# Three shared chunks ahead of the expert blocks and one beside the final sums, in place of two and two

## The chip, the cores and the metric

The kernel runs on one core of one Trainium2 chip. The metric is the device time of one execution in microseconds (us), lower being better. TensorE is called PE, VectorE DVE, ScalarE ACT, GpSimd POOL and SyncE SP below, as the profile calls them. Each engine works through its own list of instructions in the order written; between engines there are only semaphores.

## The reference, cut to what matters

A four-layer network on x of 2048 tokens by 256 features. Each layer adds an attention part and then a feed-forward part. The change lies in the last layer's feed-forward part, a mixture of 16 experts of which each token uses two, plus a shared network that every token goes through:

```python
shared = jnp.einsum('bls,ds->bld',
    jax.nn.silu(jnp.einsum('bld,sd->bls', x, sfc1)) * jnp.einsum('bld,sd->bls', x, sfc2), sfc3)
logits = jnp.einsum('bld,ed->ble', x, gate_w)
top_w, top_idx = jax.lax.top_k(logits, TOP_K)
top_w = jax.nn.softmax(top_w, axis=-1)
...
h = jax.nn.silu(jnp.einsum('td,ehd->teh', xf, w1))
moe = jnp.einsum('teh,te,edh->td', h, dispatch, w2)
return moe.reshape(B, L, D) + shared
...
x = x + jnp.tanh(g_ffn[3]) * _L3_ffn_ref(_layernorm(x, axis=-1), ...)
```

Here x is normalised, each sfc matrix has 512 hidden features, and each expert has 128.

## The kernel before, in words

The order of all work is written out by hand: for each stage there is one function for each engine. The last stage is `pe_ffn3`, `act_ffn3`, `dve_ffn3`, `pool_ffn3` and `sp_ffn3`, followed by `sp_end`. The 2048 tokens are 16 tiles of 128. All data are float32. The stage goes like this.

**Routing.** DVE picks two experts for each token and works out a slot for each of the 4096 (token, expert) pairs; the slots of one expert fill whole blocks of 128 rows, 47 blocks in all (NB3). POOL then writes the normalised tokens into a DRAM buffer xb3 by those slots: 32 indirect DMAs in `pool_scatter` (L718), one tile of one choice each.

**Shared chunks.** The shared network is made in four chunks of 512 tokens (`pe_shared`, `act_shared`, `dve_shared`, with c from 0 to 3). PE makes for each of four groups of 128 hidden features two 128x512 products (L149 is the helper `mm` that issues every matmul), ACT takes a sigmoid of the first (L2267), and DVE multiplies twice (L2274 and L2276) into HS. Then PE makes four 128x256 products, and DVE adds each, times the layer's gate, into x (L2279), which counts s_yd. Two pairs of PSUM banks alternate between the feature groups, so that PE can be two groups ahead of DVE and no more (the wait on s_hs, n - 1).

**Expert blocks.** For each of the 47 blocks SP loads 128 rows from xb3 (L2229; the first waits until all 32 scatters have landed; four buffers, so that load j waits for the transpose of block j - 4). PE transposes them (`turn`, L2296), ACT copies (`keep`, L2353), PE multiplies by the expert's first matrix, whose number it reads into a register (`up`), ACT takes the sigmoid (L2363), DVE multiplies (L2403), PE transposes again (`lift`, L2313), DVE copies (L2410), PE multiplies by the second matrix (`down`), ACT copies (L2371) and SP writes the 128 rows to a DRAM buffer yb3 (L2239). The blocks use all eight PSUM banks, so PE's shared chunks stand wholly before or behind them, and waits on s_hs and s_yd guard the change-over.

**Final sums.** When the last block has been written to yb3, POOL gathers for each tile its two expert rows: 32 indirect DMAs in `pool_gather` (L723). There are 8 buffers, so four tiles are in flight, and the gathers of tile t wait for the sum of tile t - 4 (s_fx). DVE adds each gathered tile into x with its weight (L2418), two instructions a tile, and SP then writes that tile out (L2448).

What sets the order around the change is DVE's and PE's written order. PE has chunks 0 and 1, then 47 blocks, then chunks 2 and 3. DVE has chunks 0 and 1, its share of the blocks, then chunk 2, sums of tiles 0 to 7, chunk 3, sums of tiles 8 to 15.

Of the kernel before, what the change touches and what calls it, by code (L numbers as in the profile page):

```python
# [6 lines left out]
ALU = mybir.AluOpType  # L7
# [9 lines left out]
NT = 16  # L17
# [35 lines left out]
def settle(e, own, ins):  # L53

    own.n += 1
    ins.then_inc(own.sem, 1)
    e.wait_ge(own.sem, own.n)
# [20 lines left out]
def build(nc, d, out):  # L78
    with ExitStack() as ctx:
# [12 lines left out]
        dve, act, pool = Own(sem("dve")), Own(sem("act")), Own(sem("pool"))  # L92
# [45 lines left out]
        xs = lambda t: X[:, t, :]  # L138

        s_w3, s_fx = sem("w3_in"), sem("x_out")  # L140
# [489 lines left out]
        s_gth = sems("gathered", 8)  # L630
# [112 lines left out]
        s_dn, s_yd = sem("down_prod"), sem("y_ready")  # L743
# [1470 lines left out]
        f3_Lg, f3_W12 = view(f3_w + 3200, NT, 16), view(f3_w + 3456, 2, NT)  # L2214
# [6 lines left out]
        f3_G = view(oW + 4096, 8, 256)  # L2221
# [40 lines left out]
        def act_shared(e, c):  # L2262
            for n in range(4 * c, 4 * c + 4):
                e.wait_ge(s_up, 64 + 2 * n + 1)
                if n >= 2:
                    e.wait_ge(s_hs, n - 1)
                e.activation(f3_S1[:, n % 2, :], psum[:, 2 * (n % 2) + 2, :], ACT.Sigmoid).then_inc(s_sg, 1)  # L2267
# [14 lines left out]
        def pe_ffn3(e):  # L2282
            pe_turn_logits(e, 7, lambda i: (s_xn, 113 + 2 * i + 2), xn, sml("wg3"), 16)
            pe_ranks(e, 3, 16, 32, f3_w)
            pe_totals(e, 16, 32, f3_w)
            e.wait_ge(s_w3, 32)
            e.wait_ge(s_er, 2)
            for c in range(2):
                pe_shared(e, c)

            def turn(j):
                e.wait_ge(s_rin[j % 4], RIN3[j % 4] + 16 * (j // 4 + 1))
                if j >= 2:
                    e.wait_ge(s_bx, 23 + j - 1)
                for k in range(2):
                    m = e.transpose(psum[:, j % 2, 128 * k:128 * k + 128], f3_XG[:, j % 4, 128 * k:128 * k + 128], ident)  # L2296
                m.then_inc(s_bt, 1)

            def up(j):
                e.wait_ge(s_bx, 23 + j + 1)  # L2300
                if j >= 2:
                    e.wait_ge(s_bh_, 23 + j - 1)
                regs[j] = e.value_load(ER[0:1, j:j + 1], min_val=0, max_val=15)
                for k in range(2):
                    m = mm(e, psum[:, 2 + j % 2, 0:128], f3_XGT[:, j % 3, k, :],
                           f3_W1[:, bass.ds(regs[j], 1), k, :].rearrange("p e n -> p (e n)"), k == 0, k == 1)
                m.then_inc(s_bu, 1)

            def lift(j):
                e.wait_ge(s_bh_, 23 + j + 1)  # L2310
                if j >= 2:
                    e.wait_ge(s_ba, 23 + j - 1)
                e.transpose(psum[:, 4 + j % 2, 0:128], f3_H[:, j % 2, :], ident).then_inc(s_bl, 1)  # L2313

            def down(j):
                e.wait_ge(s_ba, 23 + j + 1)
                e.wait_ge(s_bo, 23 + j - 1) if j >= 2 else e.wait_ge(s_yd, 48)
                mm(e, psum[:, 6 + j % 2, 0:256], f3_HTT[:, j % 2, :],
                   f3_W2[:, bass.ds(regs[j], 1), :].rearrange("p e n -> p (e n)"), True, True).then_inc(s_bd, 1)

            regs = {}
            e.wait_ge(s_hs, 8)
            turn(0)
            turn(1)
            e.wait_ge(s_wm, 192)
            for j in range(NB3 + 2):
                if j < NB3:
                    up(j)
                if j + 2 < NB3:
                    turn(j + 2)  # L2330
                if 1 <= j <= NB3:
                    lift(j - 1)
                if 2 <= j:
                    down(j - 2)
            e.wait_ge(s_bh_, 23 + NB3)
            e.wait_ge(s_ba, 23 + NB3)
            e.wait_ge(s_bo, 23 + NB3)
            for c in range(2, 4):
                pe_shared(e, c)

        def act_ffn3(e):
            for i in range(8):
                act_turn(e, 7, i)
            e.wait_ge(s_gx, 3)
            e.activation(f3_GW, f3_GW, ACT.Exp).then_inc(s_ge, 1)
            for c in range(2):
                act_shared(e, c)

            def keep(j):
                e.wait_ge(s_bt, 23 + j + 1)  # L2350
                if j >= 3:
                    e.wait_ge(s_bu, 46 + j - 2)
                e.activation(f3_XGT[:, j % 3, :, :].rearrange("p k n -> p (k n)"), psum[:, j % 2, 0:256],  # L2353
                             ACT.Copy).then_inc(s_bx, 1)

            keep(0)
            keep(1)
            for j in range(NB3 + 2):
                if j < NB3:
                    e.wait_ge(s_bu, 46 + j + 1)  # L2360
                    if j >= 2:
                        e.wait_ge(s_bh_, 23 + j - 1)
                    e.activation(f3_SGM[:, j % 2, :], psum[:, 2 + j % 2, 0:128], ACT.Sigmoid).then_inc(s_bg, 1)  # L2363
                if j + 2 < NB3:
                    keep(j + 2)
                if j >= 2:
                    y = j - 2
                    e.wait_ge(s_bd, 23 + y + 1)
                    if y >= 3:
                        e.wait_ge(s_rout[y % 3], ROUT3[y % 3] + 16 * (y // 3))  # L2370
                    e.activation(f3_Y[:, y % 3, :], psum[:, 6 + y % 2, 0:256], ACT.Copy).then_inc(s_bo, 1)  # L2371
            for c in range(2, 4):
                act_shared(e, c)

        def dve_ffn3(e):
            e.wait_ge(s_x, 112)
            for t in range(NT):
                dve_norm(e, 113 + t + 1, t)
            PL = psum[:, 0, 0:256].rearrange("p (t e) -> p t e", t=NT)
            e.wait_ge(s_lg, 3)  # L2380
            settle(e, dve, e.tensor_copy(f3_Lg, PL))
            OH, M_, MI = dve_top(e, f3_Lg, 16, 2, f3_w)
            e.tensor_tensor(f3_GW, M_[:, 1, :], M_[:, 0, :], ALU.subtract).then_inc(s_gx, 1)
            dve_scan(e, OH, 16, 32, f3_w)
            e.wait_ge(s_ge, 3)
            settle(e, dve, e.tensor_scalar(f3_W12[:, 0, :], f3_GW, 1.0, None, ALU.add))
            settle(e, dve, e.reciprocal(f3_W12[:, 0, :], f3_W12[:, 0, :]))
            settle(e, dve, e.tensor_scalar(f3_W12[:, 0, :], f3_W12[:, 0, :], TG[:, 7:8], None, ALU.mult))
            e.tensor_tensor(f3_W12[:, 1, :], f3_W12[:, 0, :], f3_GW, ALU.mult)
            V1 = dve_blocks(e, 2, 16, NB3, f3_w)  # L2390
            e.sem_inc(s_er, 1)
            e.wait_ge(s_rk, 3)
            dve_pick(e, OH, V1, 16, 32, f3_w, f3_SLOT)
            settle(e, dve, e.tensor_copy(f3_SLI, f3_SLOT))
            e.sem_inc(s_slot, 1)  # L2395
            for c in range(2):
                dve_shared(e, c)
            for j in range(NB3 + 1):
                if j < NB3:
                    e.wait_ge(s_bg, 23 + j + 1)  # L2400
                    if j >= 2:
                        e.wait_ge(s_bl, 23 + j - 1)
                    e.tensor_tensor(f3_H[:, j % 2, :], psum[:, 2 + j % 2, 0:128], f3_SGM[:, j % 2, :],  # L2403
                                    ALU.mult).then_inc(s_bh_, 1)
                if j >= 1:
                    y = j - 1
                    e.wait_ge(s_bl, 23 + y + 1)
                    if y >= 2:
                        e.wait_ge(s_bd, 23 + y - 1)
                    e.tensor_copy(f3_HTT[:, y % 2, :], psum[:, 4 + y % 2, 0:128]).then_inc(s_ba, 1)  # L2410
            for c in range(2):
                dve_shared(e, 2 + c)
                for t in range(8 * c, 8 * c + 8):
                    e.wait_ge(s_yd, 40 + t + 1)
                    for k in range(2):
                        s = (2 * t + k) % 8
                        e.wait_ge(s_gth[s], 96 + 16 * (t // 4 + 1))
                        m = e.scalar_tensor_tensor(out=xs(t), in0=f3_G[:, s, :], scalar=f3_W12[:, k, t:t + 1], in1=xs(t),  # L2418
                                                   op0=ALU.mult, op1=ALU.add)
                        if k == 0:  # L2420
                            settle(e, dve, m)
                    m.then_inc(s_fx, 1)

        def pool_ffn3(e):
            e.wait_ge(s_slot, 3)
# [228 lines left out]
```

## Time and profile before

| what | us |
|---|---|
| median of 3 runs | 2287.68 (2282.6 to 2291.75) |
| the profiled execution, its own time | 2269.89 |
| its span, first to last instruction | 2268.0 |
| PE busy in the span | 1811.4 (80%) |
| DVE busy | 1194.7 (53%) |
| ACT busy | 880.3 (39%) |
| POOL busy | 838.9 (37%) |
| mean granted clock of PE, share of full | 0.88 |

The rows of the profile give times from the start of the span. Busy shares are averages over stages of very different kinds; the stage in question is the last some 200 us of the span, from about 2067 us on. A timeline row gives the start, the length, the engine and line, the operation, how many instructions were merged, and in brackets how long the engine had been idle before, and what released it. PE's lengths in such a row overlap at their ends, since matmuls are pipelined. DMA_INDIRECT on POOL is the time that POOL takes to describe the transfer, which then takes its own time to land.

### The profile page before, as it was taken

What the parts mean: (1) busy time and instruction counts of PE and PEld (TensorE: products, weight loads), DVE (VectorE), ACT (ScalarE), POOL (GpSimd) and SP (SyncE); (2) the same over time, 40 slices, a digit from 0 to 9 for tenths busy, and PEclk for the clock granted to TensorE, in tenths of its full rate; (3) what the DMA queues carried; (4) which work ended last, traced back from release to release, by engine and by line L of the source; (5) the groups of instructions that cost most, each with busy time, mean ns of one, the idle gap of its engine ahead of it and who ended that gap; (6) DMA issues with size and microseconds to landing.
All of it is one profiled execution on the core that took longest, in us unless ns stands there. A gap on an engine that the chain in (4) does not pass through costs nothing.

```text
span 2268.0 us, 25730 instructions
## 1 busy us (share of the span) xinstructions
PE 1811.4 (80%) x9072; PEld 1125.0 (50%) x9072; DVE 1194.7 (53%) x2217; ACT 880.3 (39%) x1365; POOL 838.9 (37%) x805
## 2 busy tenths in 40 slices
PE   6643999908875688885899577799999899987895
PEld 3343998904653322245455345554445545555653
DVE  5942444453758466662111669656664566633334
ACT  3112433303325677741122155455453455421440
POOL 2133000071347444433000445355565456643114
PEclk9856999958977699996899899699999999987997
DMA  9112223030000000032111200000000000011443
GB/s 368 53 61 77 91 100 118 20 93 0 1 18 1 1 1 1 1 149 106 40 35 33 94 1 1 28 1 1 1 1 1 0 1 1 1 75 47 137 129 93
DMA packets 60076, 112.22 MB, mean 49 GB/s; under 512 B 7829, under 2 KB 51288, under 8 KB 57520
## 3 DMA queue, kind: packets, MB, share of 16 engines
q1 hardware_dynamic: 52272, 90.02, 11.3%
q0 software_dynamic: 7680, 20.57, 2.8%
q8 instruction: 76, 1.25, 0.2%
q14 instruction: 48, 0.39, 0.1%
HBM read 71.12 MB, written 39.80 MB: 49 GB/s over the span
## 4 chain that ended last, share of the span: by engine, by line
PE 61%; DVE 17%; POOL 9%; issue 5%; ACT 5%; DMA 3%; SPq 0%; POOLq 0%; DVEq 0%; ACTq 0%
PE psum L149 57%; POOL xb L718 3%; POOL arena L1519 2%; DVE arena L2027 2%; POOL arena L723 2%; ACT arena L1318 2%; PE psum L183 1%; DVE arena L460 1%; DVE arena L154 1%; DVE arena L164 1%; DMA arena<-yb,arena 1%; DMA arena<-xb 1%; POOL arena L620 1%; DVE arena L1400 1%; DVE rounded L759 1%
## 5 line engine op out<-in xcount | busy, mean ns | idle before, releaser
L149 PE MATMUL psum<-arena 128*128 128x512 f32 (+20 forms) x5127 | 1223.6, 468 | 178.1 <-DVE arena L1434 30.6
L149 PEld LDWEIGHTS psum<-arena 128*128 128x128 f32 (+6 forms) x5127 | 602.1, 172 | 689.1 <-issue 448.8
L149 PE MATMUL psum<-rounded 128*128 128x270 f32 (+6 forms) x2688 | 491.1, 336 | 34.6 <-DVE rounded L759 19.6
L149 PEld LDWEIGHTS psum<-rounded 128*128 128x128 f32 (+3 forms) x2688 | 382.3, 189 | 146.7 <-issue 48.0
L2100 POOL TENSOR_TENSOR arena<-arena 128x1024 f32<-128x1024 f32 (+1 forms) x112 | 270.6, 2416 | 152.7 <-ACT arena L2069 148.1
L723 POOL DMA_INDIRECT arena<-yb,arena x80 | 78.4, 980 | 390.1 <-DMA yb<-arena 343.8
L2069 ACT ACTIVATE arena<-psum 128x1024 f32<-128x1024 f32 x144 | 147.3, 1023 | 190.8 <-PE psum L149 190.1
L2027 DVE TENSOR_REDUCE arena<-psum 128x1 f32<-128x512 f32 x256 | 164.1, 684 | 86.8 <-PE psum L149 85.7
L1318 ACT ACTIVATE arena<-psum,arena 128x1024 f32<-128x1024 f32 (+1 forms) x192 | 156.3, 909 | 47.5 <-PE psum L149 47.4
L1535 POOL TENSOR_TENSOR arena<-arena 128x256 f32<-128x256 f32 x128 | 94.2, 757 | 131.5 <-ACT arena L1318 130.5
L718 POOL DMA_INDIRECT xb<-arena x80 | 80.3, 1004 | 114.9 <-DVEq L2395 37.8
L191 ACT ACTIVATE arena<-psum 128x512 f32<-128x512 f32 x56 | 32.2, 596 | 219.3 <-PE psum L183 219.3
L183 PE MATMUL psum<-arena 128*128 128x128 f32 x224 | 45.4, 355 | 81.5 <-DVE arena L964 53.7
L759 DVE SCALAR_TENSOR_TENSOR rounded<-arena,rounded 128x540 fp32r<-128x540 f32 (+1 forms) x96 | 82.0, 886 | 33.6 <-ACT rounded L889 32.1
L883 ACT ACTIVATE arena<-psum,arena 128x540 f32<-128x540 f32 x64 | 45.4, 710 | 129.9 <-PE psum L149 127.1
L159 POOL TENSOR_SCALAR arena<-arena 128x1 f32<-128x1 f32 x113 | 24.3, 215 | 177.8 <-DVE arena L155 171.9
L183 PEld LDWEIGHTS psum<-arena 128*128 128x128 f32 x224 | 36.8, 196 | 91.4 <-DVE arena L964 54.2
L1965 DVE SCALAR_TENSOR_TENSOR rounded<-psum,rounded 64x512 fp32r<-64x512 f32 (+1 forms) x80 | 47.2, 590 | 63.2 <-ACT rounded L1943 51.0
L164 DVE TENSOR_SCALAR arena<-arena 128x256 f32<-128x256 f32 x128 | 61.3, 494 | 24.7 <-POOL arena L160 23.8
L2097 POOL TENSOR_TENSOR arena<-arena 128x1024 f32<-128x1024 f32 x16 | 38.0, 2375 | 83.2 <-ACT arena L2069 83.2
L957 DVE TENSOR_TENSOR arena<-psum,arena 128x256 f32<-128x256 f32 (+1 forms) x40 | 16.9, 422 | 94.7 <-PE psum L149 94.7
L1674 POOL MEMSET arena<- 128x1 f32 x1 | 0.1, 98 | 179.8 <-DMA yb<-arena 179.8
(245 smaller groups left out, 1918.8 us busy)
## 6 DMA issues: line engine op xcount, KB each, us to landing
arena<-in_w SPq DMA_DIRECT2D x8, 2048.0 KB, 8.0
yb<-arena SPq DMA_DIRECT2D x102, 128.0 KB
xb<-arena SPq DMA_DIRECT2D x5, 2048.0 KB, 17.6
arena<-xb SPq DMA_DIRECT2D x70, 128.0 KB, 2.2
arena<-in_w1u SPq DMA_DIRECT2D x4, 2048.0 KB, 14.0
arena<-xb SPq DMA_DIRECT2D x8, 512.0 KB
arena<-in_w1d SPq DMA_DIRECT2D x1, 4096.0 KB, 13.5
arena<-in_w3b SPq DMA_DIRECT2D x1, 4096.0 KB, 12.5
```

Of the source, the lines that this page charges most:

```text
L149: return e.matmul(o, l, r, start=start, stop=stop, skip_group_check=True)
L164: e.tensor_scalar(xn(t), src(t), MV[:, t, 0:1], RS[:, t:t + 1], ALU.subtract, ALU.mult).then_inc(s_xn, 1)
L183: m = e.transpose(pt[:, t, k, :], src(2 * i + t)[:, 128 * k:128 * k + 128], ident)
L718: e.indirect_dma_start(buf, bass.IndirectOffsetOnAxis(idx[:, c:c + 1], 0), src(c % NT), None, bounds_check=bound, oob_is_err=False).then_i ...
L723: e.indirect_dma_start(dst, None, buf, bass.IndirectOffsetOnAxis(idx[:, col:col + 1], 0)).then_inc(s_gth[s], 16)
L759: e.scalar_tensor_tensor(out=dst, in0=src, scalar=1.0, in1=hi, op0=ALU.mult, op1=ALU.subtract).then_inc(sig, 1)
L1318: e.activation(PT[:, u % 3, 2 * h:2 * h + 2, 0:n], psum[:, bk:bk + 2, 0:n], ACT.Exp, bias=NBD[:, 0:1]).then_inc(s_ae, 1)
L1535: e.tensor_tensor(PT[:, u % 3, 2 * h:2 * h + 2, 0:128], PT[:, u % 3, 2 * h:2 * h + 2, 0:128], bc(cst("caus"), 1, 2), ALU.mult).then_inc(s_ ...
L1965: e.scalar_tensor_tensor(out=lo, in0=psum[r, bk, 0:64 if (kind, c) == ("k", 2) else 512], scalar=1.0, in1=hi, op0=ALU.mult, op1=ALU.subtra ...
L2027: m = e.tensor_reduce(x3_MX[:, t, a, c:c + 1], psum[:, bk, :], AX.X, ALU.max)
L2069: e.activation(x3_P[0:rows, g % 4].rearrange("p a n -> p (a n)"), psum[0:rows, bk:bk + 2, :].rearrange("p a n -> p (a n)"), ACT.Exp, scale ...
L2100: m = e.tensor_tensor(ac, ac, x3_P[0:rows, g % 4], ALU.add)
```

## The change

One more shared chunk (c = 2) is made ahead of the expert blocks, on all three engines, and only chunk 3 stays behind them. The counts that the change-over waits for rise with it (s_hs from 8 to 12, s_yd from 48 to 52). DVE's final sums, which were split in two halves with chunk 3 between them, become one run of 16 tiles behind chunk 3. Nothing is computed more or less often, and POOL's and SP's lists stay the same.

```diff
@@ pe_ffn3
-            for c in range(2):
+            for c in range(3):
                 pe_shared(e, c)
...
-                e.wait_ge(s_bo, 23 + j - 1) if j >= 2 else e.wait_ge(s_yd, 48)
+                e.wait_ge(s_bo, 23 + j - 1) if j >= 2 else e.wait_ge(s_yd, 52)
...
-            e.wait_ge(s_hs, 8)
+            e.wait_ge(s_hs, 12)
...
-            for c in range(2, 4):
-                pe_shared(e, c)
+            pe_shared(e, 3)
@@ act_ffn3
-            for c in range(2):
+            for c in range(3):
                 act_shared(e, c)
...
-            for c in range(2, 4):
-                act_shared(e, c)
+            act_shared(e, 3)
@@ dve_ffn3
-            for c in range(2):
+            for c in range(3):
                 dve_shared(e, c)
...
-            for c in range(2):
-                dve_shared(e, 2 + c)
-                for t in range(8 * c, 8 * c + 8):
-                    e.wait_ge(s_yd, 40 + t + 1)
-                    for k in range(2):
-                        s = (2 * t + k) % 8
-                        e.wait_ge(s_gth[s], 96 + 16 * (t // 4 + 1))
-                        m = e.scalar_tensor_tensor(out=xs(t), in0=f3_G[:, s, :], scalar=f3_W12[:, k, t:t + 1], in1=xs(t),
-                                                   op0=ALU.mult, op1=ALU.add)
-                        if k == 0:
-                            settle(e, dve, m)
-                    m.then_inc(s_fx, 1)
+            dve_shared(e, 3)
+            for t in range(NT):
+                e.wait_ge(s_yd, 40 + t + 1)
+                for k in range(2):
+                    s = (2 * t + k) % 8
+                    e.wait_ge(s_gth[s], 96 + 16 * (t // 4 + 1))
+                    m = e.scalar_tensor_tensor(out=xs(t), in0=f3_G[:, s, :], scalar=f3_W12[:, k, t:t + 1], in1=xs(t),
+                                               op0=ALU.mult, op1=ALU.add)
+                    if k == 0:
+                        settle(e, dve, m)
+                m.then_inc(s_fx, 1)
```

## Rows read from the trace of the kernel before

**Rows 1.** The profile's page: the span and the engines' busy time.
```profile
...
span 2268.0 us, 25730 instructions
...
PE 1811.4 (80%) x9072; PEld 1125.0 (50%) x9072; DVE 1194.7 (53%) x2217; ACT 880.3 (39%) x1365; POOL 838.9 (37%) x805
...
```

**Rows 2.** Timeline of PE, last layer: start, length, line, operation, count [idle before, releaser].
```profile
...
2106.84 7.17 PE L149 MATMUL psum<-arena 128*128 128x256 f32 x32 [0.85 <-DVE arena L2276]
2115.09 0.41 PE L2296 MATMUL psum<-arena 128*128 128x128 f32 x2 [1.08 <-DMA arena<-xb]
2115.94 0.44 PE L2296 MATMUL psum<-arena 128*128 128x128 f32 x2 [0.43 <-DMA arena<-xb]
2116.83 0.71 PE L149 MATMUL psum<-arena 128*128 x4 [0.45 <-issue]
...
2192.46 1.21 PE L149 MATMUL psum<-arena 128*128 x4
2194.30 13.97 PE L149 MATMUL psum<-arena 128*128 128x512 f32 x32 [0.63 <-issue]
...
2231.76 9.79 PE L149 MATMUL psum<-arena 128*128 128x512 f32 x16 [8.59 <-DVE arena L2276]
...
```

**Rows 3.** Chain of waits, 2110 to 2122 us: start, us, what.
```profile
...
2110.58 2.43 DMA xb<-arena
...
2113.40 2.50 DMA arena<-xb
...
```

**Rows 4.** Timeline of POOL, last layer: scatters (L718) and gathers (L723).
```profile
...
2070.81 1.11 POOL L718 DMA_INDIRECT xb<-arena  x1 [37.76 <-DVEq L2395]
...
2110.58 0.97 POOL L718 DMA_INDIRECT xb<-arena  x1 [0.30 <-issue]
2196.70 0.99 POOL L723 DMA_INDIRECT arena<-yb,arena  x1 [85.14 <-DMA yb<-arena]
...
2218.00 0.95 POOL L723 DMA_INDIRECT arena<-yb,arena  x1 [11.54 <-DVE arena L2418]
2219.25 1.13 POOL L723 DMA_INDIRECT arena<-yb,arena  x1 [0.30 <-issue]
...
2228.19 0.95 POOL L723 DMA_INDIRECT arena<-yb,arena  x1 [0.30 <-DVE arena L2418]
...
2233.19 0.95 POOL L723 DMA_INDIRECT arena<-yb,arena  x1 [0.30 <-issue]
...
2251.27 0.95 POOL L723 DMA_INDIRECT arena<-yb,arena  x1 [13.39 <-DVE arena L2418]
...
2260.20 0.95 POOL L723 DMA_INDIRECT arena<-yb,arena  x1 [0.30 <-issue]
```

**Rows 5.** Timeline of ACT, last layer: first sigmoid of chunks 2 and 3.
```profile
...
2196.29 0.60 ACT L2267 ACTIVATE arena<-psum 128x512 f32<-128x512 f32 x1 [2.20 <-PE psum L149]
...
2218.05 0.60 ACT L2267 ACTIVATE arena<-psum 128x512 f32<-128x512 f32 x1 [10.87 <-PE psum L149]
...
```

**Rows 6.** Groups of instructions, 2115 to 2194 us: PE's transposes of the expert blocks.
```profile
...
L2296 PE MATMUL psum<-arena 128*128 128x128 f32 x94 | 18.8, 283 | 2.2 <-DMA arena<-xb 2.1
...
```

**Rows 7.** By stretch: length, PE, PEld, DVE, ACT, POOL busy, clock, DMA share, GB/s.
```profile
...
2114.00:2116.00 2.00, 0.49 (x4) 0.27 (x4) 0.48 (x1) 0.38 (x1) 0.00 (x0) 1.00 0.78 240
...
2118.00:2120.00 2.00, 2.00 (x9) 2.00 (x10) 0.60 (x3) 0.80 (x3) 0.00 (x0) 0.50 0.29 67
...
2122.00:2124.00 2.00, 2.00 (x16) 1.59 (x14) 0.73 (x4) 1.66 (x6) 0.00 (x0) 1.00 0.35 97
...
```

**Rows 8.** Timeline of DVE, last layer: final sums (L2418) and chunk 3's first product (L2274).
```profile
...
2216.74 3.75 DVE L2418 SCALAR_TENSOR_TENSOR arena<-arena 128x256 f32<-128x256 f32 x8
...
2222.57 0.48 DVE L2418 SCALAR_TENSOR_TENSOR arena<-arena 128x256 f32<-128x256 f32 x1 [0.87 <-DMA arena<-yb,arena]
...
2230.20 0.68 DVE L2274 TENSOR_TENSOR arena<-psum,arena 128x512 f32<-128x512 f32 x1
...
```

**Rows 9.** Busy time and granted clock behind PE's long wait (columns as in rows 7).
```profile
...
2232.00:2235.00 3.00, 3.00 (x4) 1.23 (x5) 0.90 (x2) 0.00 (x0) 2.39 (x3) 0.50 0.47 134
...
```

## The prediction, made before the changed kernel ran

> **What bounds the kernel now.** I read the page first. The span is 2268.0 us, and PE is busy for 80% of it [rows 1]. That is an average over all layers; the change touches only the last stage, so I went to the timelines of the four engines there and asked, at each place where work leaves or arrives, who is waiting for whom.
>
> The head of the stage, PE's timeline: chunk 1's last matmuls start at 2106.84 and end 7.17 us later, at 2114.01. PE then waits 1.08 us for a DMA, transposes, waits 0.43 us for the next DMA, transposes, and starts the first expert product at 2116.83 [rows 2]. The DMAs waited for are the first loads from xb3. The chain shows why they come then: the last scatter lands 2.43 us after 2110.58, and the load takes 2.50 us from 2113.40 [rows 3]. So two shared chunks fill PE's time under the 32 scatters almost exactly. PE finishes 1.1 us before the blocks' data are there. A third chunk finds no gap to fill.
>
> The middle: PE has the expert blocks until 2193.67 (2192.46 + 1.21) [rows 2]; their timing depends on their start only.
>
> The tail: POOL's gathers start at 2196.70, 3.0 us behind PE's last block; POOL issues eight and then waits 11.54 us, until 2218.00, for the first sum, which on DVE stands behind chunk 2. From 2218.00 it issues at an even pace, and before 2251.27 it waits once more, 13.39 us, for sums that stand behind chunk 3 [rows 4]. PE, meanwhile, can run only two feature groups of chunk 3 ahead of DVE and then waits 8.59 us, until 2231.76, for it [rows 2]. So in the tail DVE's written order makes POOL and PE wait in turn. The tail is 2268.0 - 2193.67 = 74.33 us long.
>
> **The change part by part.**
>
> The price of one chunk: from chunk 2's first sigmoid to chunk 3's is 2218.05 - 2196.29 = 21.76 us, with PE the engine that sets it [rows 5].
>
> Head: chunk 2 is added between 2114.01 and the blocks, +21.76. The loads have then long landed (SP issues four without asking PE), so PE's DMA waits of 1.08 and 0.43 us go, -1.51 [rows 2]. What is late next is nothing: the second transpose, ACT's copy, the register read and the first product follow as before. Head: +20.25 us. Nothing covers it, since no other engine has work that the blocks wait for. POOL's scatters are finished, and DVE and ACT run beside PE in the chunk. SP's list is unchanged. Its four first loads are issued under the chunk, and the fifth waits for PE's first transpose as before.
>
> Within the blocks the trace could give something back. All four stalls of PE on a load come to 2.1 us, the first two (1.51) among them [rows 6]; the other 0.6 us I leave in. And PE's granted clock, at 1.00 until 2116, is at 0.50 from 2118 to 2120 (1.2 of 2.4 GHz), just behind the short waits of the change-over, and back at 1.00 by 2122 [rows 7]. With PE busy until the first transpose this dip may be gone. At most 4 us ran at half clock, so 2 us is the most that it can give back, and it is less if part of a block's time is hand-overs between engines. The new change-over still has the same small gaps between transposes and products, so I take 0 and keep 2 us for the low end.
>
> Tail, rebuilt from rows. From PE's last block to the first sum is one chunk, as now with chunk 2: 2216.74 - 2193.67 = 23.07 us [rows 2, 8]. Eight gathers have landed under it, as now. From the first sum to the ninth gather is 2218.00 - 2216.74 = 1.26 us. Then, in place of eight gathers, chunk 3 and eight more with their waits, 24 gathers run through. Twelve took 2233.19 - 2218.00 = 15.19 us beginning with the stretch in which DVE had only sums, up to 2230.20 [rows 4, 8]. That is 11 steps of 1.25 and one of 1.43. Twenty-three steps at 1.25, with 0.18 for that one, are 28.93 us. From the last gather's issue to the end is 2268.0 - 2260.20 = 7.80 us [rows 1, 4]. The sum is 23.07 + 1.26 + 28.93 + 7.80 = 61.06 us against 74.33, so -13.27 us. That contains the end of PE's wait of 8.59 us and of the half clock behind it: from 2232 to 2235, as the products of chunk 3 resume, the clock is 0.50 [rows 9].
>
> Could the sums set the pace, not POOL? Two buffers of each tile come free with its sum; tile 4's second sum ends at 2222.57 + 0.48 = 2223.05 [rows 8], and the gather that needs it is issued at 2228.19 [rows 4]. There are 5 us of slack, and it does not shrink, since eight sums cost DVE 3.75 us, 0.94 a tile [rows 8], and POOL's two gathers 2.5. PE, ACT and the yb3 writes have nothing left in that stretch. The writes of the finished tiles run beside the gathers, but they do so in the twelve-gather stretch already.
>
> **Sum:** +20.25 - 13.27 = +6.98 us. Against the profiled execution that is a span of 2268.0 + 7.0 = 2275.0, and 2269.89 + 7.0 = 2276.9 us for its own time. The median of the runs, 2287.68, lies 17.8 us above that execution, and nothing in one trace says where; I add the difference to the median: 2294.7 us, or 0.31% more. The sign comes from lost overlap: taking a chunk out of the tail gives back only 13.3 of its 21.8 us, since the rest lay beside gathers, and in front it lies beside nothing.
>
> **The rivals.**
>
> Rival 1, sums get in the way of gathers (slower still). The gather at 2219.25 took 1.13 us, not 0.95, while eight sums ran back to back on DVE [rows 4, 8]. If sums beside POOL's work cost every one of the 24 gathers that 0.18 us, not one of them, the tail is 23 x 0.18 = 4.1 us longer and the change costs +11.1 us, 2298.8 us. Against it: in the stretch after 2220 sums and gathers alternate at 1.25 us a gather. A harder form holds each of 23 gathers for a whole sum, 0.48 us [rows 8]: 7.0 + 11.0 = +18.0 us, 2305.7 us. The trace speaks for it in at most one gather of twelve. The Trainium skill ("SBUF — State Buffer", section "SBUF: two separate sides") states the harder form as a rule: while DVE runs an operation that takes both of its SBUF port pairs, GpSimd is locked out and cannot write the descriptors of its DMAs. By it the 1.13 us would be the normal case, and the twelve-gather stretch disagrees.
>
> Rival 2, the added chunk is hidden (faster). If the scatters' landing, and not PE, set the start of the blocks, chunk 2 would fill waiting time and the tail's 13.3 us would be a gain. Break-even is where the first load lands 7 us later against PE than in this trace, that is 8 us after chunk 1's end; fully hidden, at 20 us later, it would give 2287.7 - 13.3 = 2274.4 us. The 32 scatters are issued 1.28 us apart, from 2070.81 to 2110.58 [rows 4]. The unprofiled runs are 17.8 us longer than the profiled one; if 8.0 of these sat in the scatters (0.25 us in each), the change would be worth 7.0 - 8.0 = -1.0 us, 2286.7. Nothing in the trace shows such a delay: the last scatter, too, follows the one before it after 0.30 us.
>
> Rival 3, the blocks run better with their loads in hand. If the other 0.6 us of load stalls went and the clock dip's 2 us too, the change would cost 7.0 - 2.6 = +4.4 us, 2292.1. For it: four loads are ready at the start, and PE comes to the change-over without a wait. Against: from the fifth on each load still waits for a transpose, as now.
>
> **How the numbers follow.** Chances: the forecast's sum, +6 to +8 us, 0.68; rival 1 at +11 us 0.09 and at +18 us 0.03; rival 3, 0.13; rival 2, 0.07. About 0.5% (11.4 us) is what a measurement of this kernel can tell from no change, and three runs of one program spread over 9 us. The forecast lies 4.4 us inside that bound, so of its 0.68 a good 0.1 may be measured beyond it; of rival 1's 0.12 some 0.07. That gives slower by over 0.5% 0.18, faster by over 0.5% 0.04 (part of rival 2), within 0.5% 0.78. The range reaches from rival 2's break-even side, 2286, to rival 1 with the spread of the runs, 2302.
>
> **What would show it right or wrong.** In the trace of the changed kernel: PE starts the first transpose without a DMA wait some 21.8 us behind chunk 1's end; first expert product near 2137.1; PE's last block ends near 2213.9; POOL's gathers start 3 us behind it, wait once, 11.5 us, and then 24 run in 29 us; no second wait of POOL, no 8.6 us wait of PE; the clock stays at 1.00 through the last chunk. The forecast is wrong if the first transpose still waits for a load (rival 2), if many gathers take 1.1 us or are more than 1.3 us apart (rival 1), or if the 47 blocks take 2 us less than the 76.8 us from the first product to the last block's end (rival 3).

## The result and the profile after

| | us |
|---|---|
| before, median of 12 runs | 2287.87 (2282.6 to 2294.37) |
| changed, median of 12 runs | 2297.27 (2291.18 to 2303.59) |
| ratio | 1.004, 95% interval 1.0025 to 1.0055 |
| changed, profiled execution | 2295.21, span 2293.3 |

The changed kernel is slower by 0.4%, 5.7 to 12.6 us by the interval. The forecast was 2294.7 us and +7.0 us, with "within 0.5%" as the likeliest outcome. A second comparison on another chip (below) gave 1.003, 1.0009 to 1.0051.

The profile's page of the changed kernel, span and busy time, against [rows 1]: all engines have the same work to within 5 us, so the difference is waiting.

```profile
...
span 2293.3 us, 25730 instructions
...
PE 1815.7 (79%) x9072; PEld 1125.6 (49%) x9072; DVE 1196.0 (52%) x2217; ACT 879.9 (38%) x1365; POOL 840.2 (37%) x805
...
```

PE's timeline of the last stage, to be held against [rows 2]. The row with 32 products of 128x512 is where chunk 0 starts (at 2067.24 us in the first profile of before).

```profile
...
2064.88 16.99 PE L149 MATMUL psum<-arena 128*128 128x512 f32 x32 [3.69 <-issue]
2082.72 5.45 PE L149 MATMUL psum<-arena 128*128 128x256 f32 x24 [0.85 <-DVE arena L2276]
2095.34 10.27 PE L149 MATMUL psum<-arena 128*128 128x256 f32 x24 [7.17 <-issue]
2116.00 10.16 PE L149 MATMUL psum<-arena 128*128 128x512 f32 x16 [10.39 <-DVE arena L2276]
2127.01 20.91 PE L149 MATMUL psum<-arena 128*128 128x256 f32 x64 [0.85 <-DVE arena L2276]
2148.77 7.17 PE L149 MATMUL psum<-arena 128*128 128x256 f32 x32 [0.85 <-DVE arena L2276]
2155.78 0.60 PE L2296 MATMUL psum<-arena 128*128 128x128 f32 x4
2157.49 0.71 PE L149 MATMUL psum<-arena 128*128 x4 [1.11 <-ACT arena L2352]
...
2230.97 1.21 PE L149 MATMUL psum<-arena 128*128 x4
2232.81 13.97 PE L149 MATMUL psum<-arena 128*128 128x512 f32 x32 [0.63 <-issue]
2247.63 7.17 PE L149 MATMUL psum<-arena 128*128 128x256 f32 x32 [0.85 <-DVE arena L2276]
```

Three things can be read here. First, the third chunk stands ahead: the first transpose (2155.78) follows chunk 2's last product at once, with no wait for a load. Second, the tail is short: from the last block's end, 2230.97 + 1.21 = 2232.18, to the span's end are 61.1 us. Third, there is something that nobody forecast: PE waits 7.17 and 10.39 us in the middle of the chunks. POOL's gathers answer to [rows 4]: one wait of 11.52 us, and then 24 gathers in one run.

```profile
...
2235.21 0.99 POOL L723 DMA_INDIRECT arena<-yb,arena  x1 [125.96 <-DMA yb<-arena]
...
2256.51 0.94 POOL L723 DMA_INDIRECT arena<-yb,arena  x1 [11.52 <-DVE arena L2415]
...
2285.51 0.95 POOL L723 DMA_INDIRECT arena<-yb,arena  x1 [0.30 <-issue]
```

The third thing again, on the engines that PE waited for. First the waits of 2080 to 2160 us (engine, line, releaser: us in total, times, longest), where "remote" is what the profile writes when no engine or queue that it sees released the instruction; then DVE's timeline.

```profile
...
ACT arena L2267 <- remote: 33.0, 1, 33.0
...
DVE arena L2279 <- remote: 26.8, 3, 17.1
...
```

```profile
...
2085.52 0.48 DVE L2279 SCALAR_TENSOR_TENSOR arena<-psum,arena 128x256 f32<-128x256 f32 x1 [2.86 <-PE psum L149]
2094.70 0.48 DVE L2279 SCALAR_TENSOR_TENSOR arena<-psum,arena 128x256 f32<-128x256 f32 x1 [8.70 <-remote]
2112.26 0.49 DVE L2279 SCALAR_TENSOR_TENSOR arena<-psum,arena 128x256 f32<-128x256 f32 x1 [17.07 <-remote]
2113.75 0.48 DVE L2279 SCALAR_TENSOR_TENSOR arena<-psum,arena 128x256 f32<-128x256 f32 x1 [1.00 <-remote]
...
```

PE had made the products of chunk 0's first three tiles by 2088.17 (2082.72 + 5.45), about 1.7 us apart, but DVE added them at 2085, 2094 and 2112. PE needs those adds for its next tile, so its wait of 7.17 us ends with DVE's late add of the second tile. The sigmoid at 2113.80 and the one behind it had both their products by 2105.61 (2095.34 + 10.27). All this ends soon after the scatters do: POOL's last scatter is issued at 2108.27. This costs 22.5 us: from the start of chunk 0 to the end of the last chunk ahead are 91.06 us here and 68.53 us in the second profile of the same kernel. PE's two waits are 17.6 us of that; the other 5 go with the granted clock, which is at 0.50 behind both of them (2092 to 2098 and 2110 to 2122 us). So this one profile (+25.3 us on the span) is no measure of the change.

What DVE and ACT waited for can be read from the trace's record of semaphore updates. Each last matmul of an add's product raises a count (s_dn) that DVE waits for:

```text
                         matmul ends                          count raised
changed, second          2082.04 2083.77 2085.50 2087.22      2082.06 2083.78 2085.51 2087.24
changed, first           2084.71 2086.44 2088.16 2098.74      2085.50 2094.68 2112.24 2113.72
```

In the second profile the count comes 0.01 to 0.02 us behind the matmul, and so it does in the other eleven. Here it comes 0.8, 8.2, 24.1 and 15.0 us behind it, and each add starts 0.02 to 0.03 us after its count. The count that ACT waits for behaves alike: the products of chunk 1's first two feature groups end from 2100.46 to 2105.61, and all four are counted between 2113.78 and 2113.96. So DVE and ACT did not stop by themselves: PE's counts reached them late. Why they were late this does not show.

To set executions side by side, I took every profile apart at the same four marks. The start of the stage itself moves from 2062 to 2075 us between executions, whatever the kernel, since the layers ahead of it take more or less time. A comparison within the stage is free of that. "Head" is from chunk 0's first product to the first expert product, "blocks" from there to the last block's end, "tail" from there to the span's end.

```text
profile                        head   blocks   tail   stage
before, first                 49.59   76.84   74.33   200.76
before, second                49.74   76.22   74.58   200.54
before, third                 49.85   77.11   74.04   201.00
before, fourth                49.61   76.07   74.70   200.38
changed, first                92.61   74.69   61.12   228.42   (the nameless wait)
changed, second               70.08   76.66   61.15   207.89
changed, third                70.09   76.20   61.11   207.40
changed, fourth               68.57   75.05   61.11   204.73
tail alone                    49.74   76.93   61.05   187.72
woven, two and two            49.80   75.73   51.11   176.64
woven, three and one          70.09   76.71   50.96   197.76
woven, one and three          49.90   77.32   69.84   197.06
woven, one sum earlier        49.72   76.31   50.41   176.44
```

The mean stage of before is 200.67 us, and that of the changed kernel's three undisturbed profiles 206.67: +6.0 us, by head +19.9, blocks -0.6, tail -13.3.

### The profile page after: what moved, and what is told of

It is laid out like the page before. It is cut to its first block, busy times and chain, and to the rows that moved or that the text cites. A ratio compares the mean times of both kernels' runs of the same rounds, so it can differ in the third digit from the quotient of the medians.

```text
span 2293.3 us, 25730 instructions
## 1 busy us (share of the span) xinstructions
PE 1815.7 (79%) x9072; PEld 1125.6 (49%) x9072; DVE 1196.0 (52%) x2217; ACT 879.9 (38%) x1365; POOL 840.2 (37%) x805
## 4 chain that ended last, share of the span: by engine, by line
PE 63%; DVE 15%; POOL 7%; ACT 5%; issue 5%; DMA 2%; another core or an unknown queue 1%; SPq 0%; POOLq 0%; DVEq 0%; ACTq 0%
PE psum L149 59%; POOL arena L1519 2%; POOL arena L723 2%; ACT arena L1318 2%; DVE arena L2027 2%; POOL xb L718 1%; DVE arena L460 1%; PE psum L183 1%; DVE arena L154 1%; DVE arena L164 1%; DVE arena L1400 1%; POOL arena L620 1%; PE psum L530 1%; DVE rounded L759 1%
## 5 line engine op out<-in xcount | busy, mean ns | idle before, releaser
L149 PE MATMUL psum<-arena 128*128 128x256 f32 (+20 forms) x5127 | 1228.6, 469 | 185.0 <-DVE arena L1434 29.7
L149 PEld LDWEIGHTS psum<-rounded 128*128 128x128 f32 (+3 forms) x2688 | 381.8, 189 | 147.0 <-issue 48.1
L723 POOL DMA_INDIRECT arena<-yb,arena x80 | 78.5, 981 | 417.7 <-DMA yb<-arena 384.4
L718 POOL DMA_INDIRECT xb<-arena x80 | 80.5, 1007 | 115.7 <-DVEq L2393 37.8
L183 PE MATMUL psum<-arena 128*128 128x128 f32 x224 | 43.8, 346 | 80.8 <-DVE arena L964 54.0
L160 POOL TENSOR_TENSOR arena<-arena 128x1 f32<-128x1 f32 x113 | 63.2, 559 | 9.4
## 6 DMA issues: line engine op xcount, KB each, us to landing
xb<-arena SPq DMA_DIRECT2D x5, 2048.0 KB, 17.6
```

The source lines that it names most:

```text
L149: return e.matmul(o, l, r, start=start, stop=stop, skip_group_check=True)
L160: e.tensor_tensor(RS[:, t:t + 1], VE[:, t:t + 1], cst("nhalf")[:, 0:1], ALU.pow).then_inc(s_rs, 1)
L183: m = e.transpose(pt[:, t, k, :], src(2 * i + t)[:, 128 * k:128 * k + 128], ident)
L718: e.indirect_dma_start(buf, bass.IndirectOffsetOnAxis(idx[:, c:c + 1], 0), src(c % NT), None, bounds_check=bound, oob_is_err=False).then_i ...
L723: e.indirect_dma_start(dst, None, buf, bass.IndirectOffsetOnAxis(idx[:, col:col + 1], 0)).then_inc(s_gth[s], 16)
```

## The experiments

**The two kernels once more.** Both unchanged, each profiled again three times; no edit. The question was the nameless wait: does it come with the change?

Expected of the second profile of before:

> The kernel before, unchanged, profiled once more. The changed kernel's profiled execution (2293.3 us span) holds a wait that the first profile of before does not: beside the 32 scatters, from 2082 to 2113 us, DVE's adds (L2279) and ACT's sigmoid (L2267) wait 26.8 and 33.0 us for something that the profile cannot name. Theory A (the wait belongs to the stage and not to the change; the one profile of before was a lucky execution, 18 us under its own median): this execution shows the same wait in the same place, chunk 1 ends about 20 us later than in the first profile, and the span is about 2283 to 2292 us. Rival B (the third chunk brings the wait with it): this execution again has no such wait, a span near 2268 us, and chunk 1 ends 47 us after chunk 0's first product.

Measured: 2273.21 us, span 2271.4, and no such wait. PE's timeline has the stage as in [rows 2], with the wait for the first load:

```profile
...
2070.86 16.98 PE L149 MATMUL psum<-arena 128*128 128x512 f32 x32 [3.69 <-issue]
...
2118.87 0.77 PE L2296 MATMUL psum<-arena 128*128 128x128 f32 x4 [1.24 <-DMA arena<-xb]
...
2197.45 13.97 PE L149 MATMUL psum<-arena 128*128 128x512 f32 x32 [0.63 <-issue]
...
```

Expected of the second profile of the changed kernel:

> The changed kernel once more. Theory A: the wait beside the scatters is there again, or, if it comes only in some executions, its absence gives a span of about 2275 us (2268.0 + 7.0). Rival B: always there, span 2290 to 2300 us. Both: the stretch from PE's last expert block to the end is 61.1 us, as forecast.

Measured: 2271.9 us, span 2270.1, and no such wait either. PE's timeline is the one that the forecast drew; the three chunks run without a gap, the first expert product stands 70.08 us behind chunk 0's start, and the last block ends at 2208.95:

```profile
...
2062.21 16.98 PE L149 MATMUL psum<-arena 128*128 128x512 f32 x32 [3.69 <-issue]
...
2123.57 7.17 PE L149 MATMUL psum<-arena 128*128 128x256 f32 x32 [0.85 <-DVE arena L2276]
2130.58 0.60 PE L2296 MATMUL psum<-arena 128*128 128x128 f32 x4
2132.29 0.71 PE L149 MATMUL psum<-arena 128*128 x4 [1.10 <-ACT arena L2352]
...
2207.74 1.21 PE L149 MATMUL psum<-arena 128*128 x4
2209.60 13.97 PE L149 MATMUL psum<-arena 128*128 128x512 f32 x32 [0.66 <-issue]
2224.43 7.17 PE L149 MATMUL psum<-arena 128*128 128x256 f32 x32 [0.85 <-DVE arena L2276]
```

POOL's timeline of the same execution, from the ninth gather to the last: 24 gathers whose starts span 28.99 us, with one of 1.13 us and all others near 0.95.

```profile
...
2233.30 0.95 POOL L723 DMA_INDIRECT arena<-yb,arena  x1 [11.53 <-DVE arena L2415]
2234.56 1.13 POOL L723 DMA_INDIRECT arena<-yb,arena  x1 [0.30 <-issue]
2235.99 0.95 POOL L723 DMA_INDIRECT arena<-yb,arena  x1 [0.30 <-DVE arena L2415]
...
2262.29 0.95 POOL L723 DMA_INDIRECT arena<-yb,arena  x1 [0.30 <-issue]
```

The stretches around the first blocks (length; PE, PEld, DVE, ACT, POOL busy with counts; granted clock; DMA share; GB/s) answer to [rows 7]. There the clock fell to 0.50 behind the change-over, and so it did in all four profiles of before. Here it stays at 1.00, as in all four of the changed kernel:

```profile
...
2130.00:2132.00 2.00, 1.18 (x8) 0.82 (x6) 0.48 (x1) 0.66 (x2) 0.00 (x0) 1.00 0.01 4
2132.00:2134.00 2.00, 1.55 (x11) 1.33 (x12) 0.29 (x1) 0.60 (x2) 0.00 (x0) 1.00 0.42 127
2134.00:2136.00 2.00, 1.70 (x13) 1.24 (x11) 0.72 (x4) 1.15 (x4) 0.00 (x0) 1.00 0.26 74
...
```

The third and fourth profiles:

> The kernel before, a third profile, to see whether the nameless wait beside the scatters ever comes without the third chunk. Theory A: it comes or not as it did for the changed kernel (one profile of two had it); if it comes, chunk 1 ends about 20 us late. Rival B: never here. Without it the stage from chunk 0's first product to the end takes 200.5 to 200.8 us, as in the two profiles so far.

Measured: 2268.13 us, stage 201.00, no such wait.

> The kernel before, once more, for the nameless wait that one profile of three of the changed kernel had and none of three of before. Theory A (it comes rarely and with either kernel): here or not; if not, the stage takes 200.5 to 201.0 us. Rival B (it needs the third chunk): not here.

Measured: 2276.09 us, stage 200.38, no such wait.

> The changed kernel once more, for the same wait. Theory A: as rare here as with before; without it the stage takes 207.4 to 207.9 us. Rival B: it comes again in a good part of the executions, with a stage of about 228 us.

Measured: 2274.68 us, stage 204.73, no such wait. The stage is 2.7 us shorter than the expected span of values; 1.5 us of it lie in the three chunks ahead (67.03 us, against 68.53), and 1.2 in the blocks. The clock goes with the first: it is back at 1.00 some 3 us into chunk 0, against 6 us in the second profile, and 3 us more at half clock are worth 1.5.

So rival B falls as a rule: three of four profiles of the changed kernel lack the wait. Theory A is not shown either, since none of four profiles of before has it, and no execution of any other kernel here. One in four against none in four tells nothing apart. Why PE's counts came late in that execution stays open.

**Timed again.** The changed kernel, run in turn with before on another chip.

> The changed kernel again, timed in turn with the kernel before, because the first comparison (+9.4 us, interval 0.25% to 0.55%) and the forecast's +7.0 us differ by less than the spread of the runs. Theory A (the nameless wait beside the scatters comes in some executions of either kernel): a median difference of 6 to 9 us; the stage from the first product of chunk 0 to the end takes 207.8 us in an execution without that wait. Rival B (the wait comes with the third chunk): the wait is there again in this profile, and the difference is 10 us or more.

Measured: 2279.96 us against 2270.32, ratio 1.003, interval 1.0009 to 1.0051 (+2.0 to +11.6 us); stage 207.40 us in its profile. The runs of both kernels spread over 15 us or more (before 2261.6 to 2276.57, changed 2266.86 to 2284.26), so the medians' difference of 9.6 us, just above the 6 to 9 expected, is a rough figure. The ratio of 1.003 is +6.8 us, and it agrees with the stage's +6.0. The wait is absent here.

**The tail alone.** Two chunks ahead as before, chunk 2 and the 16 sums behind the blocks as in the changed kernel, and chunk 3 left out:

```diff
-            for c in range(2, 4):
-                pe_shared(e, c)
+            pe_shared(e, 2)
...
-            for c in range(2):
-                dve_shared(e, 2 + c)
-                for t in range(8 * c, 8 * c + 8):
-                    e.wait_ge(s_yd, 40 + t + 1)
+            dve_shared(e, 2)
+            for t in range(NT):
+                e.wait_ge(s_yd, min(40 + t + 1, 52))
```

> Chunk 3 is left out, so that its 512 tokens lack the shared part; two chunks stand ahead as before, chunk 2 stands behind the blocks and the 16 sums run in one piece behind it. This is the change's tail with before's head. Forecast's sum: 13.3 us faster than before (2274.5), tail 61.1 us; and since the changed kernel adds only a chunk in front, it must be slower than this by the price of a chunk in front: 20.3 us if the chunk is paid in full. Rival (the chunk in front is partly hidden by the scatters): the gap to the changed kernel is well under 20 us.

Measured: 2261.19 us against 2273.87, ratio 0.9946 (0.9924 to 0.9968), so -12.3 us by the ratio, where -13.3 was forecast; stage 187.72 against 200.67, -13.0. (The times expected of this run and the next were reckoned from the first comparison's 2287.87 us. Before ran 14 us lower here, so the differences are what can be compared.) POOL's timeline has the one wait and the run behind it:

```profile
...
2204.78 0.99 POOL L723 DMA_INDIRECT arena<-yb,arena  x1 [85.40 <-DMA yb<-arena]
...
2226.08 0.95 POOL L723 DMA_INDIRECT arena<-yb,arena  x1 [11.54 <-DVE arena L2415]
...
```

The tail is 61.05 us, the changed kernel's. The stage of the changed kernel is 19.0 us longer than this on the mean (20.2, 19.7 and 17.0 in the three undisturbed profiles, the last with the shorter head): a chunk in front is paid nearly in full. The rival of a hidden chunk falls.

**Sums woven into the chunks.** If DVE's written order is what makes POOL and PE wait, another order should take the waits away with nothing moved ahead. The two chunks behind the blocks stay there. On DVE, p is a feature group's two products, a is the add of a tile's shared part, and t is a tile's final sum:

```diff
-            for c in range(2):
-                dve_shared(e, 2 + c)
-                for t in range(8 * c, 8 * c + 8):
...
+ORDER3 = ("p8 p9 p10 t0 p11 t1 t2 a8 t3 a9 t4 a10 t5 a11 t6 p12 t7 p13 t8 p14 t9 t10 p15 t11 a12 t12 a13 t13 a14 a15 t14 t15")
...
+            for what in ORDER3.split():
+                {"p": part, "a": add, "t": total}[what[0]](int(what[1:]))
```

> Two chunks ahead and two behind as before, but DVE's 16 sums are woven between the steps of chunks 2 and 3, each near the time at which its gathers land, so that POOL never waits long for a sum and PE never long for DVE. Theory (the tail is long because DVE's written order makes POOL and PE wait in turn): the tail falls from 74.3 us to 3.0 + 31 x 1.25 + 7.8 = 49.6 us, to 53 with small slips, so 21 to 25 us faster than before, 2263 to 2267 us. Rival (gathers, sums and chunk steps get in each other's way on DVE and on SBUF when they truly run together): gathers over 1.25 us apart, tail over 60 us, gain under 14 us.

Measured: 2251.23 us against 2273.87, ratio 0.9907 (0.9882 to 0.9931), -21.1 us by the ratio; stage 176.64, -24.0. PE's timeline of the tail, and POOL's:

```profile
...
2196.18 1.21 PE L150 MATMUL psum<-arena 128*128 x4
2198.06 13.97 PE L150 MATMUL psum<-arena 128*128 128x512 f32 x32 [0.67 <-issue]
2212.88 20.91 PE L150 MATMUL psum<-arena 128*128 128x256 f32 x64 [0.85 <-DVE arena L2418]
2234.64 7.17 PE L150 MATMUL psum<-arena 128*128 128x256 f32 x32 [0.85 <-DVE arena L2418]
```

```profile
...
2200.42 0.99 POOL L724 DMA_INDIRECT arena<-yb,arena  x1 [84.25 <-DMA yb<-arena]
...
2210.58 0.94 POOL L724 DMA_INDIRECT arena<-yb,arena  x1 [0.40 <-DVE arena L2430]
...
2214.01 0.94 POOL L724 DMA_INDIRECT arena<-yb,arena  x1 [1.24 <-DVE arena L2430]
...
2240.70 0.95 POOL L724 DMA_INDIRECT arena<-yb,arena  x1 [0.30 <-issue]
```

PE makes both chunks in 43.8 us (2198.06 to 2234.64 + 7.17) without the wait of 8.59 us of [rows 2]. POOL's waits of 11.54 and 13.39 us [rows 4] have shrunk to one of 1.24 us, and the last gather is issued 43.3 us behind the last block, where it was 66.5. The tail is 51.1 us. The theory stands: before, it was the order on DVE, not an engine, that made the tail long.

**Woven, three and one; woven, one and three.** With the tail near its floor of 49.6 us, the place of the chunks can be asked anew. The edits are the change's counts (s_hs 12, s_yd 52) on the woven kernel, and the opposite (one chunk ahead, s_hs 4, s_yd 44), each with its own order of sums.

> Three chunks ahead and one behind, as in the changed kernel, with the 16 sums woven between the steps of chunk 3. Theory (with woven sums the tail is set by 32 gathers, 31 x 1.25 us and what lies around them, so a chunk behind the blocks is free and a chunk ahead costs its full 20.3 us): tail 50 to 51.5 us, as with two chunks behind (51.1), and the whole 19 to 20.5 us slower than woven two and two, so 2 to 4 us faster than before. Rival (two chunks behind still cost something beside the gathers, or a third chunk ahead is partly hidden by the scatters): the gap to woven two and two is under 17 us.

Measured: 2264.11 us against 2270.32, ratio 0.9971 (0.9951 to 0.999), -6.6 us by the ratio. That is more than the 2 to 4 us expected, but the interval (2.3 to 11.1 us) holds most of them. The stage is 197.76, -2.9 us against before. Against woven two and two it is 21.1 us longer, 0.6 more than the most expected, of which the head is 20.3 and the blocks 1.0; the tail is the same (50.96 and 51.11). PE's tail now has a single chunk, over after 22 us, and nobody gains by it:

```profile
...
2217.49 13.97 PE L150 MATMUL psum<-arena 128*128 128x512 f32 x32 [0.66 <-issue]
2232.32 7.17 PE L150 MATMUL psum<-arena 128*128 128x256 f32 x32 [0.85 <-DVE arena L2418]
```

> One chunk ahead, three behind, sums woven. Theory (the scatters, not PE, set the start of the blocks once less than two chunks stand ahead; behind them three chunks are 65 us of PE and outlast the gathers): the blocks start no earlier than 2.5 + 2.4 us behind the last scatter, where they start with two chunks ahead, within 1 us; PE is idle some 20 us ahead of them; the tail is 70 to 74 us; the whole 18 to 23 us slower than woven two and two. Rival (the blocks start earlier with PE free, or the tail hides the third chunk): under 12 us slower.

Measured: one execution of 2266.5 us, stage 197.06, 20.4 us longer than woven two and two. PE's timeline of the head shows why a chunk less in front gives nothing:

```profile
...
2067.64 16.91 PE L150 MATMUL psum<-arena 128*128 128x512 f32 x32 [3.69 <-issue]
2085.40 7.17 PE L150 MATMUL psum<-arena 128*128 128x256 f32 x32 [0.85 <-DVE arena L2277]
2115.55 1.20 PE L2297 MATMUL psum<-arena 128*128 128x128 f32 x4 [22.97 <-DMA arena<-xb]
...
```

PE is idle for 22.97 us and its first transpose stands 47.91 us behind chunk 0's start, where it stood at 47.85 with two chunks ahead in the first profile. The tail is 69.84 us, with three chunks of PE in it, 18.7 us longer than with two and just under the 70 to 74 expected. Two and two is the balance point: in front the scatters pay for two chunks, behind the gathers pay for two.

**One sum earlier.** From the woven kernel, tile 1's sum moved ahead of the fourth product (`t0 p11 t1` becomes `t0 t1 p11`).

> Woven two and two with one sum moved: tile 1's sum goes ahead of chunk 2's fourth product, since POOL waited 1.24 us for it. Theory: that wait of POOL goes and the tail falls from 51.1 to about 50 us (the floor of 49.6 by the gathers' spacing); against before the whole stays 21 to 25 us faster, and the 1 us itself can't be told in the whole. Rival (the early sum holds up chunk 2's products, and PE becomes what the end waits for): PE's rows of chunk 2 and 3 stretch, tail 51 us or more.

Measured: 2248.73 us against 2269.46, ratio 0.9888 (0.9862 to 0.9913), -25.4 us by the ratio (-20.7 by the medians); stage 176.44; tail 50.41. POOL's timeline no longer has the wait of 1.24 us, and the last gather is issued 42.66 us behind the last block, 0.65 us sooner. By the stage it is 0.2 us faster than the first woven order, which can't be told apart; these two have the shortest stages of the study.

```profile
...
2210.68 0.99 POOL L724 DMA_INDIRECT arena<-yb,arena  x1 [0.41 <-DVE arena L2430]
...
2213.22 0.94 POOL L724 DMA_INDIRECT arena<-yb,arena  x1 [0.30 <-issue]
...
2240.15 0.94 POOL L724 DMA_INDIRECT arena<-yb,arena  x1 [0.30 <-issue]
```

## Why the prediction was right, point by point

- **The gap in front.** "Two shared chunks fill PE's time under the 32 scatters almost exactly" was the step that carried the sign. It holds: with one chunk ahead PE is idle for 22.97 us and the blocks start at the same time; with three they start about 20 us later.
- **Head, +20.25 us.** Measured +20.4 us in two profiles of the changed kernel (70.08 and 70.09 against a mean of 49.70) and +18.9 in the fourth. The waits of 1.08 and 0.43 us went as forecast; the fourth's shorter head is the clock in chunk 0, which the forecast did not treat.
- **Blocks, 0 to -2 us.** The clock's dip to half behind the change-over was left in the sum, with 2 us kept for the low end. It did go, in all four profiles. The gain is clear at first: the fourteenth block's transpose stands 17.33 to 18.49 us behind the first expert product in the four profiles of before and 16.56 to 16.58 in the four of the changed kernel, 1.4 us less on the mean. Over all 47 blocks it blurs: they took 75.97 us on the mean of the three undisturbed profiles (75.65 with the first) against 76.56 for four of before, 0.6 to 0.9 us less, inside their spread of 1 to 2 us. The first profile's 74.69 by itself is the 2 us less that the prediction had named as the sign of rival 3; the others are not. So the part of rival 3 that is the clock is borne out, at a small price that the forecast had put at 0. The other part is not: waits for later loads come to 0.3 to 1.4 us in the changed kernel and 0.2 to 0.7 in before.
- **Tail, -13.27 us.** Rebuilt as 61.06 us; measured 61.12, 61.15, 61.11 and 61.11, and 61.05 with the tail alone. Nothing was off by more than 0.1 us: one wait of POOL of 11.5 us, 24 gathers over 29 us, 7.8 us from the last gather to the end.
- **Rival 1** (sums in the way of gathers) falls. Just one gather of the 24 takes 1.13 or 1.14 us, the second behind POOL's wait; before had two, one behind each of its waits. Even with sums, adds and gathers woven together, gathers take 0.94 to 1.17 us. The Trainium skill's lock ("SBUF — State Buffer", section "SBUF: two separate sides") does not show for these sums, which are 128x256 float32 and take 0.47 to 0.49 us each in every tail. For an operation with two SBUF inputs, as each of these sums has, that section of the Trainium skill names the lock only against a GpSimd operation that reads SBUF. So the prediction applied the rule more widely than it is stated, and whether a gather's issue is such a read no run here shows.
- **Rival 2** (the added chunk is hidden) falls. With two chunks ahead, and with one, the first transpose stands 47.8 to 48.1 us behind the stage's start in every profile, which is where the load has landed.
- **The sum.** +6.98 us forecast; +6.0 within the stage, +6.8 and +9.2 by the two ratios, whose intervals both hold 7. It is not right by errors that cancel: the head is 0.4 us off, the blocks 0.6, the tail less than 0.1. Adding the difference to the median of the runs gave 2294.7 against 2297.27 measured. The absolute time rests on a step that the prediction could not explain, the 17.8 us between the profile and the median; it came out because both kernels ran that much higher in the first comparison. For the profiled execution the forecast was 2276.9 against 2295.21. That miss of 18.3 us is the nameless wait of 22.5, less 2.4 for the stage's earlier start and 2.2 for the shorter blocks, and some tenths.
- **What the prediction did not see** is the cheaper cure. It named DVE's order as the cause of the long tail, and that cause could be removed where it stood.

## What to carry to other kernels

Before moving work from a place where it seems to cost waiting to another, ask at both places what other engine's time it would lie beside: here the scatters hide two chunks, the gathers hide two, and a third is paid nearly in full on either side (20.3 us in front, 18.7 behind, of 21.8). Where an engine's written order makes two others wait in turn, weave its short steps by the time at which their inputs land; that gave 21 to 25 us here, and moving the chunk cost 6 to 9. When executions differ by more than the effect, take profiles apart at marks inside the stage: the changed kernel's tail repeated to 0.1 us, and before's to 0.7, where the whole moved by 15.

## What was not expected of the hardware

In one of thirteen profiles of all kernels here, semaphore counts that PE raises reached DVE and ACT up to 24.1 us late, beside the indirect scatters. DVE waited 17.1 us for an add whose product had been there since 2088.16, ACT at least 8 us (2105.61 to 2113.80), and both went on 4.0 and 5.5 us behind the last scatter's issue. PE was held only through them, and POOL, which waited for no count in that stretch, kept its 1.28 us a scatter. No instruction fetch shows in the queues there.

Two things on record bear on the cause and do not settle it. First, that trace is poorer than the others: it holds 11660 semaphore updates and 5579 landings of DMAs, where the other twelve hold 12894 to 12931 and 6808 to 6816. Records are missing in other stages too, the tail among them, where nothing was late. Whether the recording itself took part in the delay is a rival that no run here tests. Second, this execution (2295.21 us) is no slower than the other eleven of the changed kernel in the first comparison (2291.18 to 2303.59), though the wait cost it 22.5 us, and all 24 of that comparison lie above the later ones of their kernel: before 2282.6 to 2294.37 against 2261.15 to 2277.71, changed 2291.18 to 2303.59 against 2266.86 to 2284.26. So it may be that those executions, of before too, held such a wait or something else of that size. It was not seen, since no other of them was profiled. What causes it stays open.

PE's granted clock dropped from 1.00 to 0.50 behind short waits at the change-over: one load's wait of 1.1 to 1.3 us, or two of 1.08 and 0.43 to 0.59 us, with the short gaps of the first blocks behind them [rows 2, 7]. That is so in all seven profiles with two chunks ahead, whatever the tail. In all five with three chunks ahead, PE made its first transposes straight behind the last chunk, then had one gap of 1.1 us and the same short ones, and the clock stayed at 1.00.
